# Mamba-2 layer with an expert feed-forward on one core: in the paired groups VectorE turns x to tokens by rows, in 32-wide squares, where TensorE did

## What is computed

```
proj = xn @ in_proj_w.T            -> gate (4096), hbc (4096 + 1024 + 1024), dt (64)
x, B, C = split(silu(causal_conv4(hbc)))
dt = softplus(dt + dt_bias);  dA = exp(dt * A)
state = state * dA + (dt * x) outer B        # per head, token after token
y     = state . C + x * D
out   = (rms_norm_per_group(y) * norm_weight * silu(gate)) @ out_proj_w.T
```

## Time and profile before

| what | value |
|---|---|
| median of 3 runs | 3209.19 us |
| the profiled execution itself | 3208.17 us |
| its span in the trace | 3206.4 us |
| TensorE busy | 3190.6 us |
| VectorE busy | 2059.9 us |
| ScalarE busy | 1546.5 us |
| GpSimd busy | 813.0 us |

### The profile page before, as it was taken

How to read it: one execution, slowest core, us unless ns; L and a number is a source line. 1 busy time by engine, 2 the same in 40 slices (tenths; PEclk the granted TensorE clock), 3 DMA queues, 4 the chain that set the end, 5 groups by cost and what they waited for, 6 DMA issues and landing times.

```text
span 3206.4 us, 55094 instructions
## 1 busy us (share of the span) xinstructions
PE 3190.6 (100%) x18248; PEld 2633.2 (82%) x18248; DVE 2059.9 (64%) x3429; ACT 1546.5 (48%) x3816; POOL 813.0 (25%) x917
## 2 busy tenths in 40 slices
PE   8999999999999999999999999999999999999999
PEld 7888888887888888888788888888878888888887
DVE  7987777786476665656457666665645766565653
ACT  5666666663354444444235444444513545444441
POOL 4444443443022222222103222222210212121220
PEclk9999999999999999999999999999999999999999
DMA  8777777776755555555565555555556655555554
GB/s 292 280 267 256 272 266 274 265 279 235 241 192 191 179 186 187 184 190 192 169 234 198 183 179 189 183 187 186 196 171 226 209 179 190 184 185 191 181 186 158
DMA packets 185669, 672.68 MB, mean 210 GB/s; under 512 B 21056, under 2 KB 22208, under 8 KB 185408
## 3 DMA queue, kind: packets, MB, share of 16 engines
q1 hardware_dynamic: 161280, 584.91, 53.8%
q10 hardware_dynamic: 24128, 84.42, 7.5%
HBM read 532.41 MB, written 136.84 MB: 209 GB/s over the span
## 4 chain that ended last, share of the span: by engine, by line
PE 96%; DVE 3%; ACT 0%; issue 0%; DMA 0%; ACTq 0%; DVEq 0%
PE dense L1031 27%; PE dense L1033 27%; PE dense L1032 27%; PE pY L1126 3%; PE pD L1156 2%; PE pX L1100 2%; PE pD L1126 1%; DVE conv_us L1438 1%; PE pU L1031 1%; PE dense L1068 1%; PE pCB L1103 1%; PE pU L1033 1%; PE pS L1033 1%; PE pS L1031 1%; PE pS L1032 1%; PE pU L1032 1%
## 5 line engine op out<-in xcount | busy, mean ns | idle before, releaser
L1031 PE MATMUL dense<-xn_hi,w_hl 128*128 128x512 f32 (+1 forms) x2888 | 1143.8, 396 | 0.6 <-POOL w_hl L426 0.3
L1033 PE MATMUL dense<-xn_hi,w_hl 128*128 128x512 f32 (+1 forms) x2888 | 1124.9, 390 | 0.0
L1032 PE MATMUL dense<-xn_lo,w_hl 128*128 128x512 f32 (+1 forms) x2888 | 1123.3, 389 | 0.0
L1033 PEld LDWEIGHTS dense<-xn_hi,w_hl 128*128 128x128 f32 (+1 forms) x2888 | 540.1, 187 | 116.0
L1031 PEld LDWEIGHTS dense<-xn_hi,w_hl 128*128 128x128 f32 (+1 forms) x2888 | 540.7, 187 | 113.2 <-issue 3.0
L1032 PEld LDWEIGHTS dense<-xn_lo,w_hl 128*128 128x128 f32 (+1 forms) x2888 | 541.0, 187 | 110.7 <-issue 1.9
L1438 DVE SCALAR_TENSOR_TENSOR conv_us<-conv_in,const_g,conv_us 128x512 f32<-128x512 f32 x576 | 467.2, 811 | 239.4 <-ACT conv_us L676 225.7
L1031 PE MATMUL dense<-z_hi,w_hl 128*128 128x512 f32 x1024 | 406.3, 397 | 1.7 <-DVE acc L1557 1.2
L1033 PE MATMUL dense<-z_hi,w_hl 128*128 128x512 f32 x1024 | 399.5, 390 | 0.0
L1557 DVE TENSOR_TENSOR acc<-acc,dense 128x512 f32<-128x512 f32 x256 | 175.7, 687 | 347.6 <-PE dense L1033 337.3
L1032 PE MATMUL dense<-z_lo,w_hl 128*128 128x512 f32 x1024 | 398.7, 389 | 0.0
(11 more groups left out here) (196 smaller groups left out, 4337.1 us busy)
## 6 DMA issues: line engine op xcount, KB each, us to landing
w_hl<-w_split SPq DMA_DIRECT2D x732, 512.0 KB, 3.5
w_split<-w_hl SPq DMA_DIRECT2D x244, 512.0 KB, 3.6
cum_b<-cum_scratch ACTq DMA_DIRECT2D x128, 512.0 KB, 4.6
w_raw<-w_slots_dram SPq DMA_DIRECT2D x122, 512.0 KB, 5.3
acc<-x_tr_dram ACTq DMA_DIRECT2D x16, 512.0 KB, 6.5
out_tr_dram<-acc ACTq DMA_DIRECT2D x16, 512.0 KB, 4.7
BC<-x_tok_dram SPq DMA_DIRECT2D x6, 512.0 KB, 4.8
conv_us<-x_tok_dram SPq DMA_DIRECT2D x6, 512.0 KB, 5.6
```

Of the source, the lines that this page charges most:

```text
L1031: nc.tensor.matmul(out, lhs[0], rhs[0], start=start, stop=False)
L1032: nc.tensor.matmul(out, lhs[0], rhs[1], start=False, stop=False)
L1033: return nc.tensor.matmul(out, lhs[1], rhs[0], start=False, stop=stop)
```

## The change

In paired groups, for the chunks of BY_DVE (all four), TensorE leaves out the four transposes of x. VectorE instead makes 16 transposes per chunk: each reads 32 partitions of xT, of all four channel tiles the 32 columns of a quarter chunk, transposes the four 32x32 squares, and writes them to the 32 partitions of that quarter in a new SBUF tile x_tm. `x_rows(g, c, p, first, end)` does the quarters first to end of the channel partitions, 4 instructions each; it is spread over VectorE's order. The three products read x_tm instead of pX. There is one x_tm, so the transposes of a chunk wait until the D product of the chunk before is done (`xd_done`). `out_adds` is split into its halves so that pieces of `x_rows` stand between them.

```diff
+        x_tm = sb("x_tm", [128, GC])
...
+        BY_DVE = (0, 1, 2, 3)
+
+        def xt_n(q, g, c):
+            return (q - 1) * (len(BY_DVE) * (G - 1)) + (g - 1) * len(BY_DVE) + (BY_DVE.index(c) + 1)
...
-                def chunk_1(g, c, p):
+                def chunk_1(g, c, p, x_by_dve=False):
...
-                    for j in range(XT):
-                        mm = nc.tensor.transpose(pX[:, j * 128:(j + 1) * 128], xT[p][:, j, cs], ident[:])
-                    mm.then_inc(s1, 1)
-                    nc.tensor.transpose(pCB[:, 0:N], BT[p][:, cs], ident[:])
+                    if not x_by_dve:
+                        for j in range(XT):
+                            mm = nc.tensor.transpose(pX[:, j * 128:(j + 1) * 128], xT[p][:, j, cs], ident[:])
+                        mm.then_inc(s1, 1)
+                    mm = nc.tensor.transpose(pCB[:, 0:N], BT[p][:, cs], ident[:])
+                    if x_by_dve:
+                        mm.then_inc(s1, 1)
...
+                def x_rows(g, c, p, first, end):
+
+                    if c not in BY_DVE:
+                        return
+                    n = chunk(q, g, c)
+                    if first == 0:
+                        dve.wait_ge(post, post_n(q, g, XT - 1))
+                        dve.wait_ge(xd_done, n + 1)
+                    for f in range(first, end):
+                        for k in range(4):
+                            src = xT[p][32 * f:32 * f + 32, :, c * Q + 32 * k:c * Q + 32 * k + 32]
+                            dst = x_tm[32 * k:32 * k + 32, :].rearrange("p (j i) -> p j i", j=XT)[:, :, 32 * f:32 * f + 32]
+                            ins = nc.vector.transpose(dst, src)
+                    if end == 4:
+                        ins.then_inc(xt_done, 1)
...
-                    dve.wait_ge(s1, n * 2 + 1)
-                    nc.vector.tensor_tensor(heads(dtx_2[half_of(two, c)]), heads(pX[:]), per_head(0, c), ALU.mult)\
+                    x_c = x_tm if two and c in BY_DVE else pX
+                    if two and c in BY_DVE:
+                        dve.wait_ge(xt_done, xt_n(q, g, c))
+                    else:
+                        dve.wait_ge(s1, n * 2 + 1)
+                    nc.vector.tensor_tensor(heads(dtx_2[half_of(two, c)]), heads(x_c[:]), per_head(0, c), ALU.mult)\
...
+                    x_rows(g, 0, p, 0, 4)
                     chunk_1(g, 0, True)
                     masked(g, 0, True)
...
+                    x_rows(g, 1, p, 0, 2)
                     y_state(g, 0, True)
                     y_skip(g, 0, True)
                     gate_tile(g, 3, False)
                     state(g, 0)
                     dve.wait_ge(acc_loaded, (q + 1) * 64)
-                    out_adds(g, 0)
+                    out_adds(g, 0, halves=(0,))
+                    x_rows(g, 1, p, 2, 3)
+                    out_adds(g, 0, halves=(1,))
+                    x_rows(g, 1, p, 3, 4)
                     if not last:
                         consts_next(g, p)
                     chunk_1(g, 1, True)
-                    out_adds(g, 1)
+                    out_adds(g, 1, halves=(0,))
+                    x_rows(g, 2, p, 0, 1)
+                    out_adds(g, 1, halves=(1,))
                     masked(g, 1, True)
-                    out_adds(g, 2)
+                    x_rows(g, 2, p, 1, 2)
+                    out_adds(g, 2, halves=(0,))
+                    x_rows(g, 2, p, 2, 3)
+                    out_adds(g, 2, halves=(1,))
...
                     y_intra(g, 1, True)
+                    x_rows(g, 2, p, 3, 4)
                     chunk_1(g, 2, True)
-                    out_adds(g, 3)
+                    out_adds(g, 3, halves=(0,))
+                    x_rows(g, 3, p, 0, 1)
+                    out_adds(g, 3, halves=(1,))
                     masked(g, 2, True)
+                    x_rows(g, 3, p, 1, 4)
```

More of the change, by code:

```diff
@@ L245, in layer_kernel @@
         xd_done = sem("xd_done")
+        xt_done = sem("xt_done")
         sdec_done = sem("sdec_done")
@@ L1277, in paired_group @@
                     gate_unit(g, False, 1)
-                    chunk_1(g, 0, p)
+                    chunk_1(g, 0, p, 0 in BY_DVE)
                     gate_unit(g, False, 2)
@@ L1284, in paired_group @@
                     out_units(g, 0)
-                    chunk_1(g, 1, p)
+                    chunk_1(g, 1, p, 1 in BY_DVE)
                     out_units(g, 1)
@@ L1293, in paired_group @@
                     chunk_2y(g, 1, True)
-                    chunk_1(g, 2, p)
+                    chunk_1(g, 2, p, 2 in BY_DVE)
                     out_units(g, 3)
@@ L1301, in paired_group @@
                     chunk_3(g, 1, two=True)
-                    chunk_1(g, 3, p)
+                    chunk_1(g, 3, p, 3 in BY_DVE)
                     x_units(2)
@@ L1460, in chunk_1_x @@
                         dve.wait_ge(prep_done, q * PREPS + g + 2)
-                    dve.wait_ge(s1, n * 2 + 1)
-                    nc.vector.tensor_tensor(heads(dtx_2[half_of(two, c)]), heads(pX[:]), per_head(0, c), ALU.mult)\
+                    x_c = x_tm if two and c in BY_DVE else pX
[4 more added lines that the diff above has]
+                    nc.vector.tensor_tensor(heads(dtx_2[half_of(two, c)]), heads(x_c[:]), per_head(0, c), ALU.mult)\
                         .then_inc(xw_done, 1 if updates else 2)
                     if updates:
-                        nc.vector.tensor_tensor(heads(wx[:]), heads(pX[:]), per_head(1, c), ALU.mult).then_inc(xw_done, 1)
+                        nc.vector.tensor_tensor(heads(wx[:]), heads(x_c[:]), per_head(1, c), ALU.mult).then_inc(xw_done, 1)
                 def chunk_1_rest(g, c, two=False):
                     n = chunk(q, g, c)
+                    x_c = x_tm if two and c in BY_DVE else pX
                     dve.wait_ge(ck_evac, n + 1)
@@ L1473, in chunk_1_rest @@
                         dve.wait_ge(sq_done, n + 1)
-                    nc.vector.tensor_tensor(heads(xD_2[half_of(two, c)]), heads(pX[:]), D_g[:].unsqueeze(2).broadcast_to([128, HPG, P]),
+                    nc.vector.tensor_tensor(heads(xD_2[half_of(two, c)]), heads(x_c[:]), D_g[:].unsqueeze(2).broadcast_to([128, HPG, P]),
                                             ALU.mult).then_inc(xd_done, 1)
@@ L1548, in gated_lo, with out_adds @@
                         .then_inc(z_done, 1)
-                def out_adds(g, m, tail=False):
-                    for h in range(2):
+                def out_adds(g, m, tail=False, halves=(0, 1)):
+                    for h in halves:
                         i = 2 * m + h
```

## The result

The changed kernel takes 3219.7 us (median of 8, 3219.2 to 3220.3) against 3209.1 before: ratio 1.0033, 95% interval 1.0022 to 1.0044. It is slower, by 10.6 us; 3186 was predicted, 3168 to 3214 the range. TensorE's saving came as forecast; two waits for VectorE in nearly every paired group ate more than that, and the experiments take them apart. A version with the same idea that takes 3174.2 us is among them.

What follows compares the result with a forecast made beforehand. TensorE was taken to bound the kernel: 3208.2 us, less 37 for removed transposes, plus 14 of stalls waiting for VectorE, gives 3185, or 3186 with 1.0 to the median. Forecast band 3179 to 3195, range 3168 to 3214.

Steps and rivals of the forecast that it cites:

- The bound on TensorE: TensorE, busy 3190.6 of 3206.4 us, holds 96% of the last chain; work removed there shortens the run.
- the worth of the removal: Four x transposes leave TensorE in each of 84 chunks, 0.44 us each: 37.0 us saved.
- The step of a transpose: Each of 16 VectorE transposes per chunk was priced at 0.32 us, within bounds of 0.20 and 0.46.
- The free places: Chunk 0's 16 transposes, twelve of chunk 1 and the last twelve of chunk 3 fit VectorE's idle and cost nothing.
- The first stall: Between the additions of 1048.38 and 1051.92, a product held by GpSimd's S_lo stalls TensorE 0.5 us, 0.05 in group 7.
- VectorE's chain between the two places: From 1054.1, VectorE's work of 9.2 us plus 5.1 of transposes leads to 1068.4 without holding.
- the second place: At the addition of 1067.13, VectorE ends at 1069.1 against TensorE's need at 1068.9: a stall of 0.2 us.
- One partial overlap is 0.7.: At the addition of 1067.13, GpSimd's S_dec and the two operations behind it hold VectorE's products 0.7 us in all.
- rival B: GpSimd's three operations alternate with the three products before the 1067.13 addition: 1.0 us more per group, 3207; chance 0.08.
- My argument against it: Between two waiting GpSimd operations VectorE gets in, so only one of them is usually met.
- The sign that the text set for rival C: TensorE's new waits for the output addition would come to over 1.8 us per group.
- rival C: The transpose step itself is slower: gain used up at 0.39 us, 3234 us at a step of 0.46; chance 0.15.

Runs made afterwards that it cites:

- f3: Changed kernel with one transpose per chunk instead of 16 and x_tm zeroed once, so outputs are not the layer's: 3174.6 us, ratio 0.9889.
- g1: f1 with the first half of the next group's chunk 0 transposed earlier, ahead of the loop's back edge: 3174.2 us, ratio 0.9890.
- e4: Changed kernel with each square written to the partitions it was read from, so quarters change every fourth transpose and outputs are wrong: 3181.6 us, ratio 0.9913.
- e3: Changed kernel with the transposes writing into the PSUM bank pX instead of x_tm, so the three products read PSUM: 3193.1 us, ratio 0.9951.
- f1: e3 with the copy of the next group's constants moved from before chunk 1's products to behind chunk 1's masking: 3188.0 us, ratio 0.9932.
- g2: f1 with VectorE's loop over three pairs of groups written out, so no back edge between groups: 3174.8 us, ratio 0.9892.
- g3: Changed kernel with the two loops of x_rows exchanged, so successive transposes write the same quarter and read changing ones: 3220.3 us, ratio 1.0034.
- f2: Changed kernel, x still in SBUF, with only the copy of the next group's constants moved behind chunk 1's masking: 3220.5 us, ratio 1.0033.

## Why the prediction was wrong

**Right.** The bound on TensorE and the worth of the removal: 37 us said, 35.1 measured (f3, g1). The step of a transpose: 0.32 said, 0.31 measured, and for the reason weighed, as e4 shows. The free places, and that exactly two places in a group are tight, at the additions of the earlier trace rows: 39 of TensorE's 42 new waits are there. The first stall: 0.5 said, 0.38 measured. That it came so near is in part luck: what was held was the copy of constants (1.05 instead of 0.17, beside S_lo), not the first product, and that in 12 of the 18 groups; in the groups 3 and 5 nothing or little was held, and VectorE was late from the back edge. VectorE's chain between the two places: of the 14.3 us predicted without holding, 14.4 came (from 1055.17 to the addition's end at 1071.59 are 16.4, of which 2.0 are held).

**The step that failed** is the last term of the second place: "One partial overlap is 0.7." It was two held products, 0.85 and 1.12, together 1.97. The stall there was 1.40, not 0.2, and over 21 groups that is 25 us. The mechanism was the one in the text, and the count of 1 was the mistake. It is rival B, whose price of 1.0 us per group was 0.2 too low and to which I gave 0.08. My argument against it, that a waiting VectorE operation gets in between two of GpSimd, was true and worked the other way: C_lo had to wait for wx, which put S_lo just ahead of xD, so two of the three products met one. e3 shows its size: with x in PSUM both products take 0.68, no second stall is left, and the time is 27 us shorter. The sign that the text set for rival C, waits of over 1.8 us per group, couldn't tell the two apart: 2.1 us per group were lost (1.8 in gaps alone), while the transposes cost what was forecast. What separates B from C is the length of the products and of the transposes.

**Terms left out.** A stall costs more than its gap: 0.18 and 0.14 us of slower starts behind each, some 6 us in all. And the back edge of VectorE's loop: 2.5 to 3.4 us in front of the transposes of the groups 3 and 5, which I had read as a wait for TensorE that transposes could fill. In the changed kernel these six groups are some 4 us longer, all together, than the 0.4 us per group accounts for. In f1 the back edge costs 13 us (3188.0 against 3174.8 in g2), 11 of which stand in the traced execution as six longer groups.

The sum with the measured terms: 3209.1 - 35.1 + 18 x 2.10 + 3 x 1.54 = 3216.4, with the 4 us behind the back edges 3220; 3219.7 was measured.

**The rules.** The one on quarters, of the Trainium skill ("VectorE: DVE Perf Modes", section "Two Vector instructions with no wait between them"), holds an instruction when the quarter that it reads or the one that it writes is another than last time. e4 and g3 agree with both halves: a step of 0.31 with a change of either quarter, a mean of 0.22 where three of four steps change neither. The one on the shared ports ("SBUF — State Buffer", section "Who interferes with whom") names also one-source operations like `tensor_scalar` as able to contend with GpSimd; the trace agrees, with the copy of constants at 1.05 us beside S_lo and 0.18 in f2 beside an idle GpSimd, and I had priced the copy as free.

## What to carry to other kernels

When work moves off the bounding engine, what it is worth is read from the steps of the chain, and what it costs from the two or three places where the receiving engine has to hand something back in time; sum that engine's work between such places, not over the kernel. An operand that moves from PSUM to SBUF changes who can lock whom: if it is the second SBUF operand on VectorE beside a busy GpSimd, count a hold for each operation that can meet one, not one for all, or leave the operand in PSUM. Look at the engine's idle behind loop edges before putting work there: the releaser that the profile names may hide a standstill that ends just before it.

## What the runs showed of the hardware that was not expected

- VectorE stands still for 2.3 to 3.4 us at its loop's back edge (2.5 to 3.4 in the changed kernel, 2.3 to 3.2 in f1, none in g2); six times per run here. What it does in that time stays open.
- A 32-partition transpose of four 32x32 fp32 squares costs VectorE 0.31 us where a quarter changes with each (changed kernel, g3); in e4 the steps are 0.19 to 0.24 within a quarter and 0.27 at a change. Into PSUM its mean length is 322 ns, into SBUF 302.
- A copy of 34 elements per partition between SBUF tiles took 1.05 us instead of 0.17 beside a GpSimd subtraction.
- Both engines pay where their operations meet: the products wx and xD took 1.53 and 1.80 instead of 0.68, and GpSimd's C_lo 0.91 instead of 0.46.
- TensorE's first matmuls behind a stall start 0.34 and 0.24 us apart instead of 0.23, at an unchanged granted clock.
